# Layer norm of all sixteen fronts: the normalised rows written by ScalarE instead of VectorE

## What is computed

```
def _layernorm(x, axis=-1, eps=1e-05):
    m = jnp.mean(x, axis=axis, keepdims=True)
    v = jnp.var(x, axis=axis, keepdims=True)
    return (x - m) / jnp.sqrt(v + eps)
...
x = x + tanh(g_xattn[0]) * L0_xattn(_layernorm(x), ctx)   # A: 16 heads, norm of q and k, 48 + 16 context tokens
x = x + tanh(g_ffn[0])   * L0_ffn(_layernorm(x))          # B: 16 experts (top 4) and a shared one, SwiGLU
x = x + tanh(g_xattn[1]) * L1_xattn(_layernorm(x), ctx)   # C: 16 heads of 128, masked
x = x + tanh(g_ffn[1])   * L1_ffn(_layernorm(x))          # D: SwiGLU, weights looked up in a table of 16
```

## Time and profile before

| | us |
|---|---|
| median of 3 runs | 533.88 (533.27 to 535.6) |
| span of the profiled execution | 530.4 |
| TensorE busy | 443.2 |
| VectorE busy | 362.0 |
| ScalarE busy | 199.5 |
| GpSimd busy | 170.8 |

### The profile page before, as it was taken

The page is one execution under the profiler, slowest core; times in us unless marked ns, Lnnn a source line. Parts: engine busy times, 40 slices in busy tenths (PEclk is TensorE's granted clock), DMA queues, the critical chain, the costliest instruction groups (busy, mean ns, idle before and its releaser), DMA issues.

```text
span 530.4 us, 8960 instructions
## 1 busy us (share of the span) xinstructions
PE 443.2 (84%) x2992; PEld 399.9 (75%) x2992; DVE 362.0 (68%) x785; ACT 199.5 (38%) x390; POOL 170.8 (32%) x204
## 2 busy tenths in 40 slices
PE   0575948666468999999998999989999998989996
PEld 0455837555468889898997978968998896888886
DVE  5768688695506557585757698698788779855542
ACT  2355535363221333233233534454344344423331
POOL 3004132232300221212123453564454365333322
PEclk9958886959556999999899969998996998999999
DMA  8111010100200020010201001001000100000000
GB/s 242 30 59 59 1 59 0 60 2 6 93 1 0 1 99 0 15 83 0 99 0 53 1 0 53 1 0 51 0 0 1 50 0 0 0 0 21 20 20 21
DMA packets 6628, 15.96 MB, mean 30 GB/s; under 512 B 1090, under 2 KB 4291, under 8 KB 6100
## 3 DMA queue, kind: packets, MB, share of 16 engines
q1 hardware_dynamic: 6612, 15.75, 9.1%
HBM read 14.70 MB, written 1.05 MB: 30 GB/s over the span
## 4 chain that ended last, share of the span: by engine, by line
PE 51%; issue 17%; DVE 13%; POOL 11%; ACT 4%; DMA 3%; POOLq 0%; DVEq 0%; ACTq 0%; SPq 0%
PE ps L287 34%; DVE work L1277 4%; PE ps L1071 3%; PE ps L468 3%; POOL work L1329 2%; POOL workr L1453 2%; PE ps L803 2%; POOL workA L554 2%; PE ps L458 2%; PE ps L824 2%; PE ps L827 1%; POOL wB_lo L560 1%; PE ps L258 1%; DMA stage<-in_wC 1%; PE ps L1083 1%
## 5 line engine op out<-in xcount | busy, mean ns | idle before, releaser
L287 PE MATMUL ps<-xT_hi,wB_hi 128*128 128x256 f32 x224 | 67.7, 302 | 1.7 <-POOL wB_lo L1334 1.7
L287 PE MATMUL ps<-xT_lo,wB_hi 128*128 128x256 f32 x224 | 64.6, 289 | 0.0
L287 PE MATMUL ps<-xT_hi,wB_lo 128*128 128x256 f32 x224 | 64.4, 288 | 0.0
L287 PE MATMUL ps<-wB_hi,workr 128*128 128x256 f32 (+1 forms) x224 | 52.4, 297 | 3.8 <-POOL workr L1453 3.4
L287 PE MATMUL ps<-wN_hi,shared_r 128*128 128x256 f32 x256 | 52.7, 301 | 0.0
L995 POOL TENSOR_TENSOR workr<-work,workr 128x256 fp32r<-128x256 f32 (+1 forms) x36 | 22.9, 636 | 83.8 <-ACT workr L878 83.8
L287 PEld LDWEIGHTS ps<-xT_hi,wB_hi 128*128 128x128 f32 x224 | 44.1, 197 | 4.0 <-issue 1.9
L1329 POOL TENSOR_SCALAR work<-work,lut_step,lut 128x344 f32<-128x344 int32 (+1 forms) x72 | 46.5, 660 | 1.6 <-POOL wB_lo L1334 1.6
L1277 DVE COPY_PREDICATED work<-work 128x1376 f32<-128x1376 int32 (+5 forms) x36 | 43.6, 1212 | 4.0 <-DVE work L1277 1.1
L287 PEld LDWEIGHTS ps<-wN_hi,shared_r 128*128 128x128 f32 x256 | 43.9, 206 | 1.5 <-DVE shared_r L1240 1.5
L287 PEld LDWEIGHTS ps<-xT_lo,wB_hi 128*128 128x128 f32 x224 | 44.2, 197 | 0.0
(11 more groups left out here) (178 smaller groups left out, 1161.3 us busy)
## 6 DMA issues: line engine op xcount, KB each, us to landing
stage<-in_wC SPq DMA_DIRECT2D x4, 1280.0 KB, 5.4
stage<-in_wB SPq DMA_DIRECT2D x4, 768.0 KB, 4.3
stage<-in_idx SPq DMA_DIRECT2D x4, 536.0 KB, 4.0
stage<-in_wA SPq DMA_DIRECT2D x2, 512.0 KB, 5.6
out<-x SPq DMA_DIRECT2D x4, 256.0 KB, 2.2
x<-in_x SPq DMA_DIRECT2D x1, 768.0 KB, 7.2
ctx_T<-in_ctx_T SPq DMA_DIRECT2D x1, 512.0 KB, 7.6
ctx_n<-in_ctx_n SPq DMA_DIRECT2D x4, 128.0 KB, 2.2
```

Source lines behind the costliest of these rows:

```text
L287: last = nc.tensor.matmul(out, l, r, start=start and i == 0, stop=stop and i == 2)
```

## The change

`front_norm` moves from VectorE to ScalarE. ScalarE writes `xn` = rstd * x + offset as an Identity activation per tile, with scale and offset from columns. GpSimd makes, behind the power, -mean (a multiplication by a tile of -1) and offset = -mean * rstd, both on 128x2. `front_stats` waits for the rows of the front before, since the statistics' tile is now read by other engines. The calls stand in ScalarE's functions: in the start behind the first weight cast and behind the guess of the head norm, in A between `act_A_qk` and `act_A_k`, in B behind `upper(2)`, in C behind the second half of the queries, in D behind `tanh(4)`. A memset of the tile of -1 is added to GpSimd's start.

```diff
--- before.py
+++ after.py
@@ -118,6 +118,9 @@
         rstd = sb("rstd", [P, TILES])
+        minus_one = sb("minus_one", [P, TILES])
+        minus_mean = sb("minus_mean", [P, TILES])
+        offset = sb("offset", [P, TILES])
         xT_hi = sb("xT_hi", [P, DC, TG], F32R)
@@ -199,7 +202,7 @@
-        front = signals("front", stat=4, var_ready=1, rstd_ready=1, xn_ready=2, xT_done=1, hi_ready=1, lo_ready=1)
+        front = signals("front", stat=4, var_ready=1, mean_turned=1, rstd_ready=1, offset_ready=1, xn_ready=2, xT_done=1, hi_ready=1, lo_ready=1)
         A = signals("A", dve=4, act=1, ctx_hi=2, ctx_lo=2, kv_done=2, q_done=1, kv_ready=6, q_ready=1,
@@ -229,6 +232,7 @@
                 nc.vector.bn_stats(stats[:, t, :], x[:, g * TILES + t, :]).then_inc(*front["stat"].up())
+            dve.wait_ge(*front["xn_ready"].at(f, 0))
             for t in range(TILES):
@@ -236,20 +240,21 @@
-        def front_norm(dve, f, g):
-
-            dve.wait_ge(*front["rstd_ready"].at(f, 1))
-            for t in range(TILES):
-                nc.vector.tensor_scalar(xn[:, t, :], x[:, g * TILES + t, :], mv[:, t, 0:1], rstd[:, t:t + 1],
-                                        ALU.subtract, ALU.mult).then_inc(*front["xn_ready"].up())
-
-        def front_dve(dve, f, g):
-            front_stats(dve, f, g)
-            front_norm(dve, f, g)
-
         def front_pool(pool, f):
...
             nc.gpsimd.tensor_tensor(rstd, ve, expo, ALU.pow).then_inc(*front["rstd_ready"].up())
+            nc.gpsimd.tensor_tensor(minus_mean, mv[:, :, 0], minus_one, ALU.mult).then_inc(*front["mean_turned"].up())
+            pool.wait_ge(*front["rstd_ready"].at(f, 1))
+            pool.sem_inc(waited, 1)
+            pool.wait_ge(*front["mean_turned"].at(f, 1))
+            nc.gpsimd.tensor_tensor(offset, minus_mean, rstd, ALU.mult).then_inc(*front["offset_ready"].up())
+
+        def front_norm(act, f, g):
+
+            act.wait_ge(*front["offset_ready"].at(f, 1))
+            for t in range(TILES):
+                nc.scalar.activation(xn[:, t, :], x[:, g * TILES + t, :], ACT.Identity, scale=rstd[:, t:t + 1],
+                                     bias=offset[:, t:t + 1]).then_inc(*front["xn_ready"].up())
@@ -604,6 +609,7 @@
             act_A_guess(act, 0)
+            front_norm(act, 1, 1)
             front_upper(act, 1, 7)
@@ -629,6 +635,7 @@
                 act_A_qk(act, n)
+                front_norm(act, g + 2, (g + 2) % GROUPS)
                 act_A_k(act, n)
@@ -651,7 +658,7 @@
             dve.wait_ge(x0_in, 16)
-            front_dve(dve, 0, 0)
+            front_stats(dve, 0, 0)
             dve.wait_ge(wA_hi_ready, 1)
@@ -659,7 +666,7 @@
             dve.wait_ge(ctxT_in, 16)
-            dve.wait_ge(setup_pool, 4)
+            dve.wait_ge(setup_pool, 5)
             dve_A_ctx(dve, 0)
@@ -673,7 +680,7 @@
             dve.wait_ge(x_in, 16)
-            front_dve(dve, 1, 1)
+            front_stats(dve, 1, 1)
             dve_A_scale(dve, 0)
@@ -704,7 +711,6 @@
             if more:
-                front_norm(dve, g + 2, (g + 2) % GROUPS)
                 dve_A_k(dve, n)
@@ -895,6 +901,8 @@
                 upper(k - 2)
+                if k == 4:
+                    front_norm(act, 5 + g, after(g))
                 if k in (3, 5):
@@ -970,7 +978,6 @@
             weighted(0)
-            front_norm(dve, 5 + g, after(g))
             for k in range(3, EC + 1):
@@ -1178,6 +1185,7 @@
             queries(1)
+            front_norm(act, 9 + g, after(g))
             upper_probs(0)
@@ -1277,7 +1285,6 @@
             take_bits(0)
-            front_norm(dve, 9 + g, after(g))
             shift(0, 0)
@@ -1415,6 +1422,8 @@
                 tanh(k)
+                if more and k == 4:
+                    front_norm(act, 13 + g, g + 1)
                 upper(k - 1)
@@ -1424,8 +1433,6 @@
                     front_stats(dve, 13 + g, g + 1)
-                if more and k == 3:
-                    front_norm(dve, 13 + g, g + 1)
                 n = rows_D(k)
@@ -1522,11 +1529,12 @@
             nc.scalar.copy(wA_hi[:, 0:NWC], stage[:, 0:NWC]).then_inc(wA_hi_ready, 1)
+            front_norm(act, 0, 0)
             act.wait_ge(wA2_in, 16)
...
             act.wait_ge(const_in, 16)
-            act.wait_ge(setup_pool, 4)
+            act.wait_ge(setup_pool, 5)
             act_A_start(act)
@@ -1571,10 +1579,11 @@
             nc.gpsimd.memset(expo, -0.5).then_inc(setup_pool, 1)
+            nc.gpsimd.memset(minus_one, -1.0).then_inc(setup_pool, 1)
             nc.gpsimd.memset(workAr[:, 0:4 * TG].bitcast(F32), 0.0).then_inc(setup_pool, 1)
...
             nc.gpsimd.memset(vz.rearrange("p t k b n -> p (t k b n)"), 0.0).then_inc(setup_pool, 1)
-            pool.wait_ge(setup_pool, 4)
+            pool.wait_ge(setup_pool, 5)
             pool_A_start(pool)
...
```

## The result

The changed kernel takes 538.39 us in the median of 16 runs (533.74 to 540.84); the kernel before, run beside it on the same chip, takes 533.27 (median of 16). One of these 16 runs, at 602.57 us, was far slower than the rest and is left out of the ratio. The ratio is 1.009, with a 95% interval of 1.0068 to 1.0112. By the ratio this is 4.8 us more (3.6 to 6.0; the medians differ by 5.1), slower by more than the 0.5% that a measurement can tell apart. My likeliest case was +1.95 us, within 0.5%. That case did not come. The range, which ended at 538.4, holds the time by 0.01 us.

The account below looks back on a forecast made before the run. TensorE leads (busy 84%), nearly filled in stages B and D, while stage A depends on queue places. Terms 1.0 + 0.15 + 2.1 + 0 - 1.3 + 0 = +1.95 on 533.88 gave 535.8 us; range 532.9 to 538.4.

Parts of the forecast that it names:

- likeliest case: Whole kernel: the stage terms sum to +1.95 us, giving 535.8 us, 0.4% more; chance 0.48.
- The pair at 1.07: ScalarE, each front: the two new Identity activations take 1.07 us together, with bounds 0.72 and 1.24.
- Multiplications at 0.3 each: GpSimd, behind the power: two new 128x2 multiplications take 0.3 us each, so the offset comes 0.6 later than the scale.
- Start, 1.0: First front: the pair delays the second weight cast and so TensorE's first transposes; cost 1.0 us, bounds 0.4 to 1.9.
- Second front, 0.15: Start, second front: TensorE turns the heads slightly later, at about 28.15; cost 0.15 us, bounds -0.3 to 0.9.
- Stage A, 2.1: Three passes: the pair delays the copy that releases TensorE by 0.65, 0.8 and 0.65 us; bounds 1.0 to 2.6.
- thus this goes straight into the pass: Stage A: TensorE has no other work before the copy releases it, so the delay lengthens the passes by 2.1 us.
- Stages B and D, 0: B: ScalarE's 2.01 us idle hides the pair; D: TensorE's 0.51 idle absorbs a 0.35 delay; cost 0 each.
- Stage C, -1.3: Second and fourth groups: delayed GpSimd work no longer collides with a VectorE addition; gain 0.65 us each, bounds 0 to 2.7.
- collision stays: Rival, stage C: the VectorE-GpSimd collision remains or its saving is lost, so 1.3 us is not gained: 537.1; chance 0.25.
- Dearer small operations: Rival, all fronts: multiplications at 0.69 us and a pair at 1.24 give +4.6 us, 538.5; chance 0.11.
- 3.5 around the span: Whole run: the median 533.88 us exceeds the profiled span of 530.4 by 3.5, which lies around it and stays.

Follow-up runs that it names:

- a_only: Kernel before with only the three normalisations of stage A's passes on ScalarE, behind the queries' activation: 540.45 us, ratio 1.0121.
- start_wait: Changed kernel with VectorE waiting in the start for the first front's power before its subtraction: 538.10 us, ratio 1.0076.
- before_look: Kernel before, unchanged, run again for a second profile: 534.34 us.
- changed_look: Changed kernel, with nothing altered, run again for a second profile: 539.58 us.

## Why the prediction was right and wrong

**The forecast of the result** (+1.95, within 0.5%): the range just holds the time, the likeliest case is wrong. Measured +4.8. By the rows and runs: start 1.5 to 1.6, place in stage A 1.8, clock in stage A 1.6 for one stretch or 3.2 for two, stage C -1.4. This sums to 3.5 to 5.2. Both profiles of the changed kernel have one stretch; two are seen only in profiles of a_only and start_wait, which have the same stage A. That the range holds the time is luck: by 0.01 us, and only because the kernel before took 533.27 in that run and not the 533.88 from which I counted. Its upper end was +4.5, below the measured +4.8, and it was drawn there for dearer operations, which did not come.

**The pair at 1.07:** right, 1.08 to 1.09. **Multiplications at 0.3 each:** free they take 0.20; with VectorE in the way up to 1.23 in stage A. I had named that block, and there it had the cover that I gave it. In the start ScalarE does wait for the last of them (2.39 us before the pair), as my sum had it.

**Start, 1.0:** mis-sized, 1.54. The mechanism, the cast behind the waiting pair, was right. I had priced the power at its old 0.69. I applied the rule that VectorE and GpSimd shut each other out to stage C and to stage A's scaling, and not to the start, although L656, a subtraction of two SBUF tiles, stood right behind the instructions that I took away. **Second front, 0.15:** within its bounds, at -0.17. From VectorE's L405 (21.85 before; L410 at 24.38 after) to the turning of the heads it is 6.15 us before and 5.98 after. The rest of this execution's lag there arose ahead of it, and before_look has it too.

**Stage A, 2.1:** the failed step. As a shift of the copy it was right within what profiles can tell: 1.8 against one profile of before, 1.2 against the other. The step that fails is "thus this goes straight into the pass". A delay of TensorE's work was priced at its length only. In the second pass TensorE's idle time before L473's product was 0.67 and became 1.25 (1.31 in changed_look), and in both profiles of the changed kernel a stretch at 1.2 GHz came behind it, 1.6 us each. The kernel with the filler, which keeps the delay and loses the stretch, is 3.5 us faster (1.6 to 5.4). Where I looked at the clock, I looked only for gains from shorter idle times in stage C.

**Stages B and D, 0:** right as to the place; the idle time before the tanh fell from 2.01 to 1.02. The profiled stage B is 0.9 us longer with a stretch at the lower clock, which a_only has too with B unchanged.

**Stage C, -1.3:** right in size (-1.4), in mechanism, and in place for the second group (0.72 in the rows above). For the rest the two medians agree with 2 x 0.7. The rival "collision stays", at 0.25, did not come: L1341 starts 0.40 after L1295, not before it. The margin was as thin as I wrote.

**The rivals.** "Dearer small operations" (538.5) has the right time for the wrong reason: the pair was not dear, nor were the multiplications where the sum counted them; what was dear in the start was the power, by 0.84. No rival of mine was the clock.

**"3.5 around the span":** wrong. The changed kernel's run had 535.68 - 533.9 = 1.8 around its span. With the same 1.8, the profile of before belonged to an execution of some 532.2 us (an estimate: 530.4 + 1.8), shorter than the median. This did not move the forecast, since both were compared at the median.

**Open:** why a_only loses 1.5 to 3 us more than its stage A shows; and what decides in which pass, and how often, the stretch comes, since 1.51 us of idle time had none behind it and 1.01 had one. The changed kernel's runs spread over 7 us; its two profiles, 3.9 us apart, have one stretch in stage A each and differ most in stage C (175.96 and 180.68 us), so the spread is not explained either.

## What to carry to other kernels

Where TensorE works in bursts, price a delay ahead of a burst twice: its length, and as a risk a stretch at the lower clock, here 1.6 us each. Read the clock of every pass and of more than one execution, since the length of the idle time alone did not tell whether the stretch came. Put moved work where the engine already waits, not behind the first of two handovers: stage A's pairs cost 4.6 us (2.7 to 6.4) at one place and 0.8, which the intervals do not tell from nothing, one call earlier. When an instruction leaves VectorE, ask what starts earlier in its stead, and whether GpSimd is working then.

## What the hardware showed that I had not expected

- Two GpSimd instructions on 128x2 numbers, 0.69 and 0.20 us when free, took 1.53 and 1.08 beside one VectorE subtraction of two SBUF tiles. Waiting for the first of them only moved the block to the other.
- An idle time of 1.25 us for 0.67 was followed by some 3 us at 1.2 GHz in dense work; one of 1.51 us in the next pass was not. With four superfluous transposes, 0.5 us of work per pass, the profile shows no such stretch and the kernel is faster.
- The kernel before, run again, differs from itself by 0.65 us within stage A, by 0.90 ahead of it and by 0.65 in stage C; two profiles of the changed kernel differ by 4.7 in stage C. A lag between two profiles that is smaller than this says nothing.
